# The mask's load moves to ScalarE's DMA queue, and the keys' half of Wkv is loaded ahead of the first context

## The reference, cut to what matters

```
x = x + tanh(g_xattn) * LN(attend(LN(LN(x)), context, mask) @ Wo)
x = x + tanh(g_ffn)   * expert_of_each_token(LN(x))

attend: cn = LN(context);  q = xn @ Wq;  k, v = split(cn @ Wkv)     # 16 heads of 64
        one learned null key and null value stand ahead of the 1500
        sim  = where(mask, (q * 0.25) . k, -max);  out = softmax(sim) . v
```

## Time and profile before

| what | value |
|---|---|
| median of three runs | 767.17 us (765.58 to 769.77) |
| span of the profiled execution, first to last instruction | 761.7 us |
| PE busy | 718.0 us (94%) |
| DVE busy | 639.2 us (84%) |
| ACT busy | 497.5 us (65%) |
| POOL busy | 378.4 us (50%) |
| chain that ended last | PE 73%, ACT 9%, DVE 8%, issue 4%, DMA 3%, POOL 2% |
| mean granted clock of TensorE | 0.980 |
| data loads on SP's queue (q1) | 22325 packets, 27.18 MB |
| data loads on ScalarE's queue (q10) | 432 packets, 0.10 MB |

### The profile page before, as it was taken

How to read it: one execution, slowest core, us unless ns; L and a number is a source line. 1 busy time by engine, 2 the same in 40 slices (tenths; PEclk the granted TensorE clock), 3 DMA queues, 4 the chain that set the end, 5 groups by cost and what they waited for, 6 DMA issues and landing times.

```text
span 761.7 us, 15607 instructions
## 1 busy us (share of the span) xinstructions
PE 718.0 (94%) x5425; PEld 459.4 (60%) x5425; DVE 639.2 (84%) x1139; ACT 497.5 (65%) x639; POOL 378.4 (50%) x427
## 2 busy tenths in 40 slices
PE   2689999999999999999999999999999999999997
PEld 2646565556565756565656565756565555567886
DVE  4775989897989898979997999798979795886776
ACT  1506675766676757666766676757666766787885
POOL 3734936773737273727372737373727216366200
PEclk9858999999999999999999999999999999999999
DMA  5411021211010101010101010101000002010000
GB/s 160 126 41 42 0 74 49 74 48 44 25 42 24 41 24 41 24 41 24 41 24 41 24 40 25 41 24 41 24 0 24 2 25 56 25 26 3 4 11 14
DMA packets 22794, 27.77 MB, mean 36 GB/s; under 512 B 10109, under 2 KB 17301, under 8 KB 22757
## 3 DMA queue, kind: packets, MB, share of 16 engines
q1 hardware_dynamic: 22325, 27.18, 11.6%
q10 hardware_dynamic: 432, 0.10, 0.1%
HBM read 26.65 MB, written 0.52 MB: 36 GB/s over the span
## 4 chain that ended last, share of the span: by engine, by line
PE 73%; ACT 9%; DVE 8%; issue 4%; DMA 3%; POOL 2%; SPq 0%; ACTq 0%; DVEq 0%; POOLq 0%
PE S L1183 24%; PE A L1203 22%; PE X L1252 11%; ACT S L629 3%; DVE PP L909 3%; PE S L1351 3%; PE A L1368 3%; ACT PP L634 2%; PE X L1212 2%; DMA early<-in_Wkv_dram 2%; DVE mneg L986 1%; PE X L1368 1%; PE A L1130 1%; PE X L1262 1%; DVE mx L965 1%
## 5 line engine op out<-in xcount | busy, mean ns | idle before, releaser
L629 ACT ACTIVATE S<-S,mb 125x896 f32<-125x896 f32 x192 | 187.7, 977 | 176.3 <-PE S L1183 176.3
L909 DVE TENSOR_TENSOR PP<-S,PP 125x896 f16<-125x896 f32 x192 | 209.2, 1090 | 53.5 <-ACT PP L634 49.2
L965 DVE TENSOR_REDUCE mx<-X 128x1 f32<-128x500 f32 x336 | 211.3, 670 | 5.6 <-PE X L1252 3.6
L1203 PE MATMUL A<-PP,zh 125*128 125x448 f16 x768 | 208.3, 352 | 0.0
L634 ACT ACTIVATE PP<-S 125x896 f16<-125x896 f32 x192 | 175.1, 912 | 4.9
L1252 PE MATMUL X<-zTh,qh 128*128 128x500 f16 x336 | 133.3, 402 | 5.9 <-DVE mx L965 3.9
L1203 PE MATMUL A<-PP,zl 125*128 125x448 f16 x384 | 126.2, 352 | 0.0
L1203 PEld LDWEIGHTS A<-PP,zh 125*128 125x128 f16 x768 | 72.4, 98 | 60.7
L1183 PE MATMUL S<-qh,zTh 128*125 128x448 f16 x384 | 105.6, 356 | 3.4 <-DVE PP L909 2.3
L1183 PE MATMUL S<-qh,zTl 128*125 128x448 f16 x384 | 104.0, 352 | 0.0
L1183 PE MATMUL S<-ql,zTh 128*125 128x448 f16 x384 | 103.9, 352 | 0.0
(11 more groups left out here) (207 smaller groups left out, 1309.3 us busy)
## 6 DMA issues: line engine op xcount, KB each, us to landing
raw<-ctx_dram SPq DMA_DIRECT2D x16, 750.0 KB
Rb<-r_scratch SPq DMA_DIRECT2D x16, 448.0 KB, 3.6
wst<-in_w_dram SPq DMA_DIRECT2D x16, 256.0 KB, 3.7
early<-in_Wkv_dram SPq DMA_DIRECT2D x2, 512.0 KB, 14.1
early<-in_Wq_dram SPq DMA_DIRECT2D x1, 512.0 KB, 5.3
Wo_s<-in_Wo_dram SPq DMA_DIRECT2D x1, 512.0 KB, 12.2
x_s<-x_dram SPq DMA_DIRECT2D x1, 448.0 KB, 4.1
out_dram<-xn SPq DMA_DIRECT2D x2, 224.0 KB, 2.5
```

The source lines that it names most:

```text
L629: act.activation(s, s, ACT.Exp, bias=mb[:, p, c:c + 1]).then_inc(e_done, 1)
L909: dve.tensor_tensor(Pl[:, k, :].rearrange("p (a r) -> p a r", a=2), S[0:CK, 2 * (c % 2):2 * (c % 2) + 2, 0:HR], Ph[:, k, :].rearrange("p ( ...
L965: dve.reduce_max(mx3[:, t, blk:blk + 1], X[:, j % 2, 0:KB], AX).then_inc(mx_red, 1)
L1203: ins = mm(A[:, a, 0:HR], z[:, p, c, :], q[:, k, a * HR:(a + 1) * HR], start=(c == 0 and n < 2), stop=(c == NC - 1 and n >= 4))
```

## The change

The line that loads the keys' half of Wkv moves ahead of the load of the first context on SP's queue, and the mask's load leaves SP's queue and is issued by ScalarE, behind its three small loads. Nothing else differs.

```diff
         def _(sp):
             sp.dma_start(x_s[:, :, :], x_v).then_inc(ld_x, 16)
             sp.dma_start(Wq_s, Wq).then_inc(ld_wq, 16)
+            sp.dma_start(Wkv_s[:, 0:INNER], Wkv[:, 0:INNER]).then_inc(ld_wk, 16)
             sp.dma_start(raw[:, 0], ctx_v[0]).then_inc(ld_ctx[0], 16)
-            sp.dma_start(Wkv_s[:, 0:INNER], Wkv[:, 0:INNER]).then_inc(ld_wk, 16)
-            with nc.allow_non_contiguous_dma("the mask's 12-byte runs"):
-                sp.dma_start(mask_s[:, :, :], mask.rearrange("b (p c) -> p b c", c=NC)).then_inc(ld_m, 16)
             sp.dma_start(Wkv_s[:, INNER:2 * INNER], Wkv[:, INNER:2 * INNER]).then_inc(ld_wv, 16)
             sp.dma_start(raw[:, 1], ctx_v[1]).then_inc(ld_ctx[1], 16)
             sp.dma_start(Wo_s[:, :, :], Wo.rearrange("(t p) n -> p t n", p=128)).then_inc(ld_wo, 16)
...
             act.dma_start(cols_s[:, :], cols).then_inc(ld_cols, 16)
             act.dma_start(idf[:, :], ident_f32).then_inc(ld_idf, 16)
             act.dma_start(idh[:, :], ident_f16).then_inc(ld_idh, 16)
+            with nc.allow_non_contiguous_dma("the mask's 12-byte runs"):
+                act.dma_start(mask_s[:, :, :], mask.rearrange("b (p c) -> p b c", c=NC)).then_inc(ld_m, 16)
```

## The result

The changed kernel takes 774.14 us (median of 11 runs, 767.94 to 775.79) against 767.17 us (median of 11, 763.57 to 769.77): 7.0 us slower by the medians. The record's ratio, an estimate over all the runs, is 1.0074 with a 95% interval of 1.0053 to 1.0095, which is 4.1 to 7.3 us (the quotient of the medians alone is 1.0091). Two of the eleven runs, 767.94 and 769.97, stand apart: their granted clock was 0.977 and 0.978, that of the nine others, 773.11 to 775.79, was 0.965 to 0.971. The profiled execution is one of the nine; it took 775.66 us with a span of 773.9, so 1.8 us lie around the span. That corrects the prediction's 5.5: the profile of before (761.7) shows an execution near 763.5, as short as the shortest of its eleven, and the 12.2 us between the two spans are more than the two kernels differ by.

The account below looks back on a forecast made before the run. PE (94% busy) bounds the loop; the head is bound by Wo's landing and the first context's landing plus DVE's work. The head's +5.3 us, with 0 after it, on 767.17 gave 772.5 us, range 766.0 to 775.5.

Parts of the forecast that it names:

- The mask on ScalarE's queue: In the head: mask runs alternate with SP's packets, the mask lands at 30.3, DVE waits 7 us, head 5.3 us late.
- One packet each in turn: On the slow DMA engines: the two queues alternate, so the mask's 400 runs per engine need 400 turns.
- Rival 2: On the DMA engines: more than 12 mask runs a turn, all out by 15.6, DVE never waits; 766.5 us, chance 0.14.
- Rival 1: On the queues: SP's next issue stays held behind the mask's runs; about +0.5 us, 767.7 us, chance 0.22.
- Rival 3: In the first pass: the clock's full level comes several us earlier; near 768.5 us together with the forecast, chance 0.07.
- rival 4: On ScalarE: it is held until the mask's runs are out, Wq's copies come 20 us late; near 785 us, chance 0.02.
- Keys' weights ahead of the context: In the head: the context lands 1.5 us later by this order, bounds 1.3 to 2.3, with nothing gained.
- The sum for the head: In the head: PE's context transposes wait for DVE's split, which ends at 35.7 instead of their start at 30.38: +5.3 us.
- After the head: In the loop: the first pass follows the queries, so the head's delay goes to the end; further effects taken as 0.
- The base: Whole kernel: the median of the runs is 5.5 us over the span of 761.7, giving 767.17 as the starting time.

Follow-up runs that it names:

- mask_act: The changed kernel with the first context ahead of the keys' weights again, so only the mask moves to ScalarE's queue: 775.5 us, ratio 1.01.
- mask_long_runs: The changed kernel with the mask loaded in 125 runs of 192 bytes in place of 2000 of 12: 766.98 us, ratio 1.0001.
- experts_late: The changed kernel with the first two experts' loads issued behind the null scores' move: 770.63 us, ratio 1.0054.
- keys_first: The kernel before with only the keys' weights moved ahead of the first context, the mask staying on SP's queue: 765.83 us, ratio 0.9976.
- reorder: The kernel before with the values' weights and Wo ahead of the mask on SP's queue, the second context behind it: 768.99 us, ratio 1.0027.
- with the wait: POOL's Anl waits for DVE's mneg: added to the kernel before, 758.62 and 758.52 us; to the changed kernel, 764.36 and 763.59.
- spread: The kernel before with both first contexts and the mask loaded in 112 + 13 partitions, SP's queue reordered: 768.62 us, ratio 1.0024.
- spread_gate: The kernel before with the 112 + 13 partition loads, SP's queue reordered, and POOL's Anl waiting for mneg: 754.02 us, ratio 0.9837.

## Why the prediction was right, point by point

- **The mask on ScalarE's queue.** Right, mechanism and size. One packet each in turn: 40 and 40. 400 turns per slow engine: SP's queue ran dry just before 28.5 (predicted 28.9), 699 runs were left for the five engines, 140 each (predicted 170), the mask landed at 29.8 (predicted 30.3), and DVE idled 6.03 us (predicted 7). `mask_act` puts all of the loss on this half, `mask_long_runs` takes it away by fewer runs, `experts_late` shows that SP's packets pace it.
- **One packet each in turn.** 40 and 40 in 2 us are 8 of each for each of the five engines, and 3 and 3 in 0.2 us leave no room for batches, so the measurement decides for one each, beside packets of 6 and 4 KB. Beside smaller ones, which go to more engines (769 of SP's and 305 runs from 23 to 25 us, at a DMA share of 1.00), the turns of the five are not shown apart; by the time SP's queue ran dry, some 260 runs had gone on each (400 less 140), for the 230 packets of my count. Rival 2 is out: DVE did wait, 6.03 us.
- **Rival 1, one generator for both queues.** Refuted: SP's issue of the values' weights ended at 3.27, while the mask's runs were out only at 29.5.
- **Rivals 3 and 4.** ScalarE was not held: its mask issue took 0.58 us, and Wq's first copy stood at 7.89 (8.01 before), so rival 4 is out. Rival 3, the forecast with the clock's full level earlier, was put near 768.5; its 6 us are the first pass's 17.07 us of PE at a granted clock of 0.50 less DVE's 10.84. No run shows that much: in `mask_long_runs`, where the full level came earlier, the way from the queries to the first item's scores was 2.4 us shorter than before. The two runs at 767.94 and 769.97, with the higher granted clock (0.977 and 0.978), look like it, but no profile shows them.
- **Keys' weights ahead of the context.** The sum was near (the context 2.36 us later, 1.8 predicted), the cause wrong. The order costs 0.46 us (`keys_first`); the rest comes with the hold's end, when the values' weights and Wo share the DMA with the context (15.30 in `mask_act`; 15.41 in `reorder`, where the mask stays on SP's queue, so that its runs are not the cause). I had seen that hold as a loss alone; it also kept the way free for the context.
- **The sum for the head.** +5.3 predicted, +4.55 at the queries. Two terms were too large, by about the same. The mask came 0.47 us earlier than predicted, and DVE's way from it to the split's end, 5.4 us, became 4.95 (29.83 to 34.78): the copy of line 852 took 0.18 us (0.43 before) and `zl` 1.45 (1.66 before). In the kernel before, POOL's halves of x ran beside both; in the changed one they were over at 27.0, though POOL's own split ran beside `zl`. Which of POOL's instructions lengthens which of DVE's here is not shown.
- **After the head.** I took the loop as following one to one, with the runs' spread as noise. That was wrong, though within the range: of the 12.2 us between the two profiles, 4.33 lie in the head and 7.9 behind it, and with the wait the stretch behind the head is equal (694.2 to 694.9 us). So the change doesn't slow the loop by itself; the collisions of `mneg` and `Anl` do. They cost 8.0 and 7.7 us in the kernel before (766.62 against 758.62, 766.19 against 758.52), and by the ratios some 10 in the changed one and some 14 with the spread loads. A sign of it stood in my rows: line 976, over 128x7 numbers too, took 2.15 us beside an instruction of POOL. I priced that one line in the head (it became 2.36) and didn't look for its like in the loop. Why a head that starts at another time gives another number of collisions stays open; in most of the rows, less than 0.3 us between the starts of the two instructions decides. That the forecast of 772.5 came near 774.14 is in part luck: the head was predicted 0.75 us too long, and the loop's part was not in the sum.
- **The base.** I took 5.5 us around the span; it is 1.8, and the profile of before shows an execution shorter than the median. Since I added differences to the median, it did no harm.

## What to carry to other kernels

The mask's many tiny runs weren't hidden by moving them to another queue: where the two queues got one packet each in turn (40 and 40 from 12.5 to 14.5 us), its 400 runs per engine were out only at 29.5, 1 us after SP's queue had run dry. So look at who waits for the last byte of such a transfer (DVE, 6.03 us), and try fewer runs (766.98 us with 125) or more engines (SP's longest hold was 5.46 us in `spread`, 12.56 before). A hold on a queue may also be what keeps a later transfer out of the way of an earlier one: the context landed at 13.13 with the hold and at 15.30 without it. And before a few us in a head are hunted, look whether a short instruction in the loop has two durations, as `mneg` has with 0.17 and up to 1.89 us: here one more wait on a neighbour with slack was worth some 8 us, and the best order and shape of the loads found here 4.5 on top of it.

## What the runs showed that was not expected

- A DVE instruction over 128x7 numbers takes 0.17 us, or up to 1.89 us if POOL's two-input instruction over 128x896 started ahead of it (by 0.74 us at most, in `spread`); with POOL made to start second, all 16 together take 3.4 to 4.0 instead of 11.9 to 21.1 us.
- A load of 125 partitions of 6 KB used 0.32 of the sixteen DMA engines; cut into 112 and 13 partitions it used all sixteen (1.05), and the context landed 2.6 us earlier (1.8 in `spread_gate`).
- PE's clock stayed at its lower level (granted 0.50) from 27.8 to 65.3 us of the changed kernel, through the end of its head and the first pass, with PE busy for 28.95 of the 37.5 us. The kernel before had a mean of 0.67 from 27.8 to 38, with PE busy for 7.66 of 10.2 us, and the lower level in the first pass. In these two profiles that made little difference to the first pass: from the queries to the first item's scores it took 28.60 us after and 28.81 before. The stretch of after, then that of before, columns as in rows 4:

```profile
27.80:65.30 37.50, 28.95 (x140) 17.53 (x141) 27.95 (x57) 8.73 (x15) 17.62 (x19) 0.50 0.08 23
```
```profile
27.80:38.00 10.20, 7.66 (x84) 6.58 (x84) 5.14 (x18) 5.80 (x9) 8.95 (x15) 0.67 0.21 66
```
